# Group 0's roundings in turns, W1 in four transfers, group 1 two tiles at once, and the mean product of batch 1 at the end of group 2

## What is computed

```python
x_mean = jnp.mean(x, axis=1, keepdims=True)
fused = jnp.concatenate([x, x_mean * ones_L, hidden[:, None, :] * ones_L], axis=-1)
out = x + jax.nn.relu(jnp.einsum('bld,do->blo', fused, W) + b)
```

## Time and profile before

| | us |
|---|---|
| runs | 103.11, 103.53, 103.65 (median 103.53) |
| profiled execution | 103.63, of which the span of the trace is 101.7 |
| TensorE busy | 97.2 of 101.7 (96%), 523 matmuls |
| VectorE / ScalarE / GpSimd busy | 83.0 / 47.1 / 38.9 |
| DMA | 21.39 MB, mean 210 GB/s |

### The profile page before, as it was taken

The page is one execution under the profiler, slowest core; times in us unless marked ns, Lnnn a source line. Parts: engine busy times, 40 slices in busy tenths (PEclk is TensorE's granted clock), DMA queues, the critical chain, the costliest instruction groups (busy, mean ns, idle before and its releaser), DMA issues.

```text
span 101.7 us, 1713 instructions
## 1 busy us (share of the span) xinstructions
PE 97.2 (96%) x523; PEld 78.5 (77%) x523; DVE 83.0 (82%) x148; ACT 47.1 (46%) x116; POOL 38.9 (38%) x35
## 2 busy tenths in 40 slices
PE   5989999999999999999999999999999999999980
PEld 2348999988888786888888886888888886888870
DVE  3172789899899899999999984999999993996670
ACT  3285435895418279496397001874744003710000
POOL 1029800000000002999848500568578059950000
PEclk9999999999999999999999999999999999999999
DMA  1999999999999998999999388000591690299994
GB/s 38 269 303 290 273 268 282 273 251 266 318 256 231 269 251 221 246 234 226 345 331 286 106 195 219 0 0 0 113 267 32 134 259 20 67 283 273 248 325 144
DMA packets 35438, 21.39 MB, mean 210 GB/s; under 512 B 2020, under 2 KB 33128, under 8 KB 35432
## 3 DMA queue, kind: packets, MB, share of 16 engines
q1 hardware_dynamic: 33848, 20.13, 77.4%
q10 hardware_dynamic: 1584, 1.18, 3.9%
HBM read 12.91 MB, written 8.39 MB: 209 GB/s over the span
## 4 chain that ended last, share of the span: by engine, by line
PE 90%; DMA 4%; ACT 1%; DVE 1%; ACTq 0%; issue 0%
PE ps_y L472 77%; PE ps_y L573 4%; PE ps_y L575 4%; PE ps_y L574 4%; DMA xa<-in_x_dram 4%; PE ps_mean L491 1%; PE ps_const L540 1%; ACT xh L267 1%; DVE ps_xt L341 1%; ACT w1h L260 1%; DVE w L462 0%; ACTq L160 0%; PE ps_y L596 0%
## 5 line engine op out<-in xcount | busy, mean ns | idle before, releaser
L240 POOL TENSOR_TENSOR xa<-xa,back 128x512 f32 (+1 forms) x26 | 33.5, 1318 | 44.7 <-DVE back L354 44.7
L472 PE MATMUL ps_y<-xh,w1h 128*128 (+2 forms) x128 | 43.6, 368 | 0.4 <-ACT w1h L260 0.3
L472 PE MATMUL ps_y<-xl,w1h 128*128 (+2 forms) x128 | 43.0, 363 | 0.0
L472 PE MATMUL ps_y<-xh,w1l 128*128 (+2 forms) x128 | 42.8, 363 | 0.0
L267 ACT ACTIVATE xh<-ps_xt 128x512 fp32r<-128x512 f32 (+1 forms) x36 | 19.7, 549 | 17.4 <-DVE ps_xt L341 17.4
L472 PEld LDWEIGHTS ps_y<-xh,w1h 128*128 128x128 f32 x128 | 22.6, 189 | 5.4 <-issue 1.1
L347 DVE TENSOR_TENSOR xl<-ps_xt,xh 128x512 fp32r<-128x512 f32 (+1 forms) x36 | 22.1, 617 | 4.9 <-ACT xh L267 4.9
L472 PEld LDWEIGHTS ps_y<-xh,w1l 128*128 128x128 f32 x128 | 22.6, 189 | 3.8
L472 PEld LDWEIGHTS ps_y<-xl,w1h 128*128 128x128 f32 x128 | 22.7, 189 | 3.6
L341 DVE STREAM_TRANSPOSE ps_xt<-xa 128x512 f32<-128x512 f32 (+1 forms) x36 | 22.3, 642 | 3.6 <-DMA xa<-in_x_dram 3.3
L285 ACT ACTIVATE relu_t<-ps_y,bias 128x512 f32<-128x512 f32 x20 | 13.5, 686 | 16.8 <-DVE bias L388 15.3
(11 more groups left out here) (35 smaller groups left out, 37.1 us busy)
## 6 DMA issues: line engine op xcount, KB each, us to landing
xa<-in_x_dram SPq DMA_DIRECT2D x60, 128.0 KB, 3.8
out_dram<-xa SPq DMA_DIRECT2D x28, 256.0 KB, 4.1
w<-in_L_cond_W_dram SPq DMA_DIRECT2D x4, 256.0 KB, 5.5
w<-in_L_cond_W_dram SPq DMA_DIRECT2D x2, 512.0 KB, 6.7
w<-in_x_dram SPq DMA_DIRECT2D x4, 256.0 KB, 4.6
out_dram<-w SPq DMA_DIRECT2D x3, 256.0 KB, 3.4
xa<-in_x_dram ACTq DMA_DIRECT2D x4, 128.0 KB, 4.4
w<-in_L_cond_W_dram SPq DMA_DIRECT2D x4, 64.0 KB, 3.4
```

Of the source, the lines that this page charges most:

```text
L240: nc.gpsimd.tensor_tensor(rows, rows, back[:, t], ALU.add).then_inc(added, 1)
L472: return nc.tensor.matmul(ps_y[:, t, ls], lhs, rhs, start=start, stop=stop, skip_group_check=True)
```

## The change

1. ScalarE rounds piece k and block k of W1 in turns from k = 0. Of block 0 it rounds only tiles 0 and 1; VectorE rounds tiles 2 and 3 between its transposes of pieces 1 and 2. TensorE waits for VectorE's half at t = 2 of its first step, GpSimd before its first remainder.
2. W1's blocks 2 and 3 are loaded in transfers of their own, with a semaphore each. The second half of group 0's x is loaded by SyncE alone, behind W1. The cond transfers move behind x1, and the transpose of cond on VectorE behind group 1's pieces.
3. TensorE computes group 1's tiles 0 and 1 together, k outside, then tiles 2 and 3 one by one. ScalarE saves tile 1 of group 0 earlier.
4. `mean_bias(1)` moves from behind tile 2 to the end of group 2, and `sum_bias(1)` on VectorE from in front of turn_back(2) to in front of turn_back(4). Two more tiles (0 and 1 of group 2) are saved, into W1's own buffer, which is no longer read by then; ScalarE does it in front of relu(4), and TensorE's group 3 waits for these saves where it waited for their relus.
5. TensorE's loop over groups 3 to 6 is written out.

```diff
--- before.py
+++ after.py
@@ -65,7 +65,7 @@
     tiles = [(g, t) for g in range(LAST) for t in range(NK)]
 
     DVE_ADDS = 2
-    SAVED = H * NK
+    SAVED = H * NK + 2
 
     def steps_of_x(n, ahead):
 
@@ -84,6 +84,9 @@
 
 
     bias_line = nc.dram_tensor("bias_line", [D], F32).ap()
+
+
+    DVE_T = NK // 2
 
     def by_tile(rows):
         return rows.rearrange("p (j t m) -> p t j m", j=NQ, t=NK)
@@ -135,12 +138,12 @@
 
         x0_landed = [sem(f"x0_landed{h}") for h in range(2)]
         x_landed = [sem(f"x_landed{g}") for g in range(G)]
-        w1_landed = [sem(f"w1_landed{k}") for k in range(NK - 1)]
+        w1_landed = [sem(f"w1_landed{k}") for k in range(NK)]
         w2_landed, w3_landed = sem("w2_landed"), sem("w3_landed")
         cond_landed, b_landed = sem("cond_landed"), sem("b_landed")
         stored = sem("stored")
         warm_zeroed, cond_zeroed, ones_set = sem("warm_zeroed"), sem("cond_zeroed"), sem("ones_set")
-        w1h_ready, w1l_ready = sem("w1h_ready"), sem("w1l_ready")
+        w1h_ready, w1h_rest_ready, w1l_ready = sem("w1h_ready"), sem("w1h_rest_ready"), sem("w1l_ready")
         cond_spread, const_summed, const_ready = sem("cond_spread"), sem("const_summed"), sem("const_ready")
         halves_summed, bsum_ready = sem("halves_summed"), sem("bsum_ready")
         w2x_step = sem("w2x_step")
@@ -176,6 +179,10 @@
 
         last_x = w3[:].rearrange("p r k o -> p (r k) o")
 
+        def place(n):
+
+            return w1[:, n - RELU_RING] if RELU_RING <= n < SAVED else relu_t[:, n % RELU_RING]
+
         def store_last(eng, r, cols, added_steps):
             eng.wait_ge(last_added, added_steps)
             eng.dma_start(out_rows[LAST, :, r, cols], last_x[:, r, cols]).then_inc(stored, 16)
@@ -187,12 +194,13 @@
             load_x0(sp, 0, LOW)
             load_w1(sp, 0, 1, LOW)
             load_w1(sp, 1, 2, LOW)
-            load_w1(sp, 2, NK, LOW)
-            load_x0(sp, 1, LOW)
+            load_w1(sp, 2, 3, LOW)
+            load_w1(sp, 3, 4, LOW)
+            load_x0(sp, 1, ORDER)
+            load_x(sp, 1, ORDER)
             sp.wait_ge(cond_zeroed, 1)
             for j in range(NQ):
                 sp.dma_start(cond_c[Q * j:Q * j + B], cv[j].rearrange("b (m k) -> b m k", k=CK)).then_inc(cond_landed, 16)
-            load_x(sp, 1, ORDER)
             load_x(sp, 2, ORDER)
             load_w2(sp, ORDER)
             for j in range(NQ):
@@ -230,8 +238,10 @@
             nc.gpsimd.memset(cond_c[:], 0.0).then_inc(cond_zeroed, 1)
 
             for k in range(NK):
-                pool.wait_ge(w1_landed[min(k, NK - 2)], 16 * NQ)
+                pool.wait_ge(w1_landed[k], 16 * NQ)
                 pool.wait_ge(w1h_ready, k + 1)
+                if k == 0:
+                    pool.wait_ge(w1h_rest_ready, 1)
                 nc.gpsimd.tensor_tensor(as_tiles(w1l[:, k]), by_tile(w1[:, k]), as_tiles(w1h[:, k]),
                                         ALU.subtract).then_inc(w1l_ready, 1)
             def residual(g, t, n):
@@ -252,12 +262,13 @@
             nc.scalar.activation(act_warm[:], ones[:, 0:1], ACT.Relu)
             load_w1(act, 0, 1, HIGH)
             load_w1(act, 1, 2, HIGH)
-            load_w1(act, 2, NK, HIGH)
-            load_x0(act, 1, HIGH)
+            load_w1(act, 2, 3, HIGH)
+            load_w1(act, 3, 4, HIGH)
 
             def w1_high(k):
-                act.wait_ge(w1_landed[min(k, NK - 2)], 16 * NQ)
-                nc.scalar.activation(as_tiles(w1h[:, k]), by_tile(w1[:, k]), ACT.Copy).then_inc(w1h_ready, 1)
+                act.wait_ge(w1_landed[k], 16 * NQ)
+                ts = slice(0, NK if k else DVE_T)
+                nc.scalar.activation(as_tiles(w1h[:, k])[:, ts], by_tile(w1[:, k])[:, ts], ACT.Copy).then_inc(w1h_ready, 1)
 
             def x_high(n):
 
@@ -269,36 +280,35 @@
 
             def save(n):
                 act.wait_ge(y_ready, n + 1)
-                nc.scalar.activation(relu_t[:, n % RELU_RING], ps_y[:, n % Y_BANKS], ACT.Copy).then_inc(y_saved, 1)
+                if n >= RELU_RING:
+                    act.wait_ge(w1l_ready, NK)
+                nc.scalar.activation(place(n), ps_y[:, n % Y_BANKS], ACT.Copy).then_inc(y_saved, 1)
 
             def relu(n):
                 g, t = tiles[n]
-                products, slot = ps_y[:, t], n % RELU_RING
+                products = ps_y[:, t]
                 if n < SAVED:
                     act.wait_ge(y_saved, n + 1)
-                    products = relu_t[:, slot]
+                    products = place(n)
                 else:
                     act.wait_ge(y_ready, n + 1)
                     act.wait_ge(turned_back, n + 1 - RELU_RING)
                 if n % (H * NK) == 0:
                     act.wait_ge(bias_ready, g // H + 1)
-                nc.scalar.activation(relu_t[:, slot], products, ACT.Relu,
+                nc.scalar.activation(place(n), products, ACT.Relu,
                                      bias=bias[:, g // H, t, g // H:g // H + 1]).then_inc(relu_done, 1)
 
-            x_high(0)
-            x_high(1)
-            w1_high(0)
-            w1_high(1)
-            for k in range(2, NK):
+            for k in range(NK):
                 x_high(k)
                 w1_high(k)
             for n in range(NK, pieces_to(H) - 2):
                 x_high(n)
             save(0)
+            save(1)
             x_high(pieces_to(H) - 2)
             x_high(pieces_to(H) - 1)
-            for n in range(1, NK):
-                save(n)
+            save(2)
+            save(3)
             n_x = pieces_to(H)
             x_high(n_x)
             x_high(n_x + 1)
@@ -314,8 +324,12 @@
             x_high(n_x + 2)
             x_high(n_x + 3)
             n_x += NK
-            assert n_x == pieces_to(SLOTS) and SAVED == 2 * NK
+            assert n_x == pieces_to(SLOTS) and SAVED == 2 * NK + 2
             for n in range(len(tiles)):
+                if n == 4:
+
+                    save(2 * NK)
+                    save(2 * NK + 1)
                 relu(n)
                 for _n in range(steps_of_x(n, 2)):
                     x_high(n_x)
@@ -351,7 +365,7 @@
                 dve.wait_ge(relu_done, n + 1)
                 if n >= BACK_RING:
                     dve.wait_ge(added, n + 1 - BACK_RING)
-                nc.vector.transpose(back[:, n % BACK_RING], relu_t[:, n % RELU_RING].rearrange("p (lb om) -> p lb om", om=Q)
+                nc.vector.transpose(back[:, n % BACK_RING], place(n).rearrange("p (lb om) -> p lb om", om=Q)
                                     ).then_inc(turned_back, 1)
 
             def mean_terms(b):
@@ -404,12 +418,18 @@
             for p in (0, P // 2):
                 nc.vector.memset(two_rows[p:p + 1], 1.0).then_inc(rows_set, 1)
             turn_x(0)
-            turn_and_split(0, pieces_to(1))
+            turn_x(1)
+            dve.wait_ge(w1_landed[0], 16 * NQ)
+            nc.vector.tensor_copy(as_tiles(w1h[:, 0])[:, DVE_T:NK], by_tile(w1[:, 0])[:, DVE_T:NK]).then_inc(w1h_rest_ready, 1)
+            x_low(0)
+            turn_x(2)
+            turn_and_split(1, 2)
+            turn_and_split(2, pieces_to(1))
+            turn_x(pieces_to(1))
+            turn_and_split(pieces_to(1), pieces_to(H))
 
             dve.wait_ge(cond_landed, 16 * NQ)
             nc.vector.transpose(cond_t[:], cond_c[:].rearrange("p m k -> p k m")).then_inc(cond_spread, 1)
-            turn_x(pieces_to(1))
-            turn_and_split(pieces_to(1), pieces_to(H))
             turn_x(pieces_to(H))
             turn_and_split(pieces_to(H), pieces_to(H + 1))
             mean_terms(0)
@@ -424,7 +444,7 @@
             mean_terms(1)
             n_x = pieces_to(SLOTS)
             for n in range(len(tiles)):
-                if n == 2:
+                if n == NK:
                     sum_bias(1)
                 elif n == NK * (H + 1):
                     sum_bias(2)
@@ -515,6 +535,8 @@
                             mm(t, ls, w1l[:, k, t], xh[:, 0, k, ls], stop=True).then_inc(y_ready, 1)
                         break
                     for t in range(NK):
+                        if half == 0 and k == 0 and t == DVE_T:
+                            pe.wait_ge(w1h_rest_ready, 1)
                         mm(t, ls, w1h[:, k, t], xh[:, 0, k, ls], start=(half == 0 and k == 0))
                     pe.wait_ge(xl_ready, NK * half + k + 1)
                     for t in range(NK):
@@ -526,7 +548,16 @@
                 if half == 0:
                     group0_low(half, NK - 1)
 
-            for t in range(NK):
+
+            for k in range(NK):
+                pe.wait_ge(xl_ready, pieces_to(1) + k + 1)
+                for t in (0, 1):
+                    if k == 0:
+                        pe.wait_ge(y_saved, t + 1)
+                    last = product(1, k, t)
+                    if k == NK - 1:
+                        last.then_inc(y_ready, 1)
+            for t in (2, 3):
                 pe.wait_ge(y_saved, t + 1)
                 tile(1, 1, t)
 
@@ -551,21 +582,21 @@
```

(28 more changed lines are left out.)

## The result

The changed kernel takes 104.26 us (median of 21 runs, 103.50 to 105.08) against 103.61 us for the kernel before (21 runs, 103.03 to 104.52). The ratio is 1.0064, 95% interval 1.0041 to 1.0086: **slower by 0.6%**, where 0.7% faster was forecast. The range of 102.4 to 103.8 does not hold it.

The account below looks back on a forecast made before the run. The prediction took TensorE's almost unbroken matmuls as the bound, with gain only before 9.8 us: 103.63 - 0.71 (0.39 first product, 0.32 W1's block 2) = 102.92, with the median 0.10 lower: 102.85 us, range 102.4 to 103.8.

Parts of the forecast that it names:

- Step 7: TensorE's loop written out: the back edge lies in a stretch without a gap, so nothing to gain.
- The sum's sentence: After the front: nothing behind 9.8 us absorbs the 0.71 us gain, since TensorE is the chain to the end.
- Step 6: Later mean product and two more saves: relu(10) has 0.7 us slack, saves are done in time, nothing on the path.
- Steps 1 and 2: Front: roundings in turns start the first product 0.39 us earlier; loading W1's block 2 by itself removes a stall, 0.32.
- Step 3: Second half of group 0's x on SyncE: 3.8 us latency taken, landing at 10.7, 0.9 us of slack.
- Step 4: SyncE's longer queue: w3 issued 1.9 us later, lands at 33.0, wanted at 33.4, no stall.
- Rival B: w3 lands late: stall of 0.3 to 0.8 us before the constant's products, 103.1 to 103.6 us; chance 0.20.
- Step 5: Group 1, two tiles at once: no time by itself, but avoids a 0.3 us stall and so keeps the front's gain.
- Rivals C: W1's block 2 lands no earlier, so 0.63 of the 0.71 us is lost: 103.5 us; chance 0.10.
- D: Second half of group 0's x keeps its 5.7 us latency: stall 0.9 us, 103.7 us; chance 0.09.
- E: A SyncE issue blocked 3 us in front of w3: stall up to 3.7 us, 103.7 to 106.5 us; chance 0.09.
- parts 1 to 5: Edits of the prediction's first five steps: all but the mean product's move, two more saves and written-out loop; 0.71 us gain.

Follow-up runs that it names:

- e4: Kernel before with only TensorE's loop over groups 3 to 6 written out; 104.23 us, 1.0074.
- d1: e4 with 5 needless waits ahead of each of the last group's first 12 products, behind the fetch; 104.00 us, 1.0064.
- d2: e4 with 11 needless waits ahead of each product of group 2, so the block comes earlier; 103.36 us, 0.9998.
- b2: e4 with 30 more instructions, needless waits in groups 1 and 2 ahead of the fetch; 103.72 us, 1.0013.
- b1: Kernel before, loop kept, with 24 needless waits ahead of each tile of group 1 and 10 ahead of each product of group 2; 104.00 us, 1.0058.
- e3: Kernel before with the mean product's move, the two more saves and the loop written out; 104.71 us, 1.0101.
- b4: Changed kernel with 30 needless instructions in groups 1 and 2, ahead of the fetch; 103.16 us, 0.9965.
- b3: e1 with 30 needless instructions in groups 1 and 2, ahead of the fetch; 103.02 us, 0.9948.
- e1: Changed kernel with batch 1's mean product in the middle of tile 3 of group 2, not at the group's end; 103.77 us, 0.9989.
- d3: c1 with batch 1's mean product moved by one product, into tile 3 of group 2; 103.30 us, 0.9974.
- c4: b3 with group 1 computed tile by tile as before; 103.46 us, 1.0003.
- f1: e1 with 11 needless waits ahead of each product of group 2; 102.96 us, 0.9937.
- c1: Changed kernel with the mean product's move and two saves undone and TensorE's loop kept; 103.26 us, 0.9994 to the kernel before.
- c2: e1 with the turn-backs of two more tiles ahead of the mean's terms on VectorE; 104.55 us, 1.0134.
- c3: b3 with the turn-backs of two more tiles ahead of the mean's terms on VectorE; 103.36 us, 0.9990.

## Why the prediction was wrong, by its own steps

**Step 7, the loop written out, costed at 0, is the step that failed.** It asked only whether the back edge stalls TensorE, found that it doesn't (the trace before still says so), and stopped there. What the longer program adds is one more block of instructions, and what that costs hangs on when it comes: at 87 us some 0.7 us (e4: 1.0074; d1: 1.0064), at 77 to 85 us nothing (d2: 0.9998; b2: 1.0013). It shows in the landing of the last store. The page of before showed three such packets, in a row that was passed over; dividing the program's length by the 256 instructions that the Trainium skill gives to a block (same section), and asking which stretch the next fetch falls in, would have found it. (902 instructions had three packets, 1030 in b1 and 1077 four, which fits.) The Trainium skill's rule on taken branches, named beside the step, speaks for unrolling and led away from it; the other one of that section ("Runtime: NRT & Kernel Launch", Instruction fetch mechanics), that crossing into a new block is mostly hidden, holds for a block at 77 or 85 us here and not for one at 87.

**The sum's sentence that nothing behind 9.8 us absorbs the gain, since TensorE is the chain to the end,** was wrong in two places. The chain ends in stores, not in TensorE; SyncE's wait for the last 128 KB was never looked at, and it varies from 1.4 to 2.7 us among these profiles, more than the whole forecast gain. And the chain left TensorE at 41.8 us.

**Step 6, "nothing on the path", was wrong by about 0.3 us.** It followed relu(10) and the saves, which were right (TensorE has no such wait in the profile). It did not follow VectorE's queue to its end in that group of work: the terms of batch 2, which had 1.17 us of slack before. The product's end moved from about 40.0 to 42.2, VectorE stood idle 0.62, and 0.73 us reached the terms. TensorE's lead of 0.61 and VectorE's lag of 0.73 together are 1.34, against 1.17 of slack: a wait of 0.17; 0.24 was measured. The step had what was needed: its own lead of 0.71 and its own "about 1 us later" for VectorE come to 1.7 against the 1.17 that the trace before shows, a wait of 0.5. e3 against e4 puts it at 0.3%, b4 against b3 at 0.2%, each within overlapping intervals, e1 at 0.4 to 0.75%.

**Steps 1 and 2 were right, a little large.** First product 6.79 (forecast 6.67), fourth step 9.25 without a stall (9.15), half 1 at 12.61 (12.51): 0.61 us of the 0.71. Over the profiles of all kernels here, half 1 starts at 13.18 in the mean with the old order (8 kernels) and at 12.63 with the new (12), so 0.55 is typical. The stall that step 2 removes differs between executions: with the old order the fourth step starts anywhere from 9.53 (d2) to 10.20 (b2). **Step 3**: x's second half landed in 3.4 to 3.6 us, better than the 3.8 taken. **Step 4**: w3 was issued at 25.3 and 25.8, 1.8 later as forecast, and landed in 5.1 to 7.3; no stall in the profile of the changed kernel nor in nine others, one of 0.6 us in d3. Rival B was priced right, and one profile in eleven does not contradict the 0.20 it got. **Step 5** holds (c4). Rivals C, D and E did not come about; the slower side had been given to E, a blocked issue, and came by a mechanism that no rival named.

**The sum with the measured terms**, in per cent: the best version, without a late block and with the mean product in the middle, is -0.6 (f1); a late block +0.4 to +1.4 (four pairs; 0.66 between d1 and d2); the mean product at the end of group 2 +0.2 to +0.4. That gives 0.0 to +1.2, and +0.64 was measured: it fits, but is no sharp check, and the changed kernel itself is in one of the pairs. That parts 1 to 5 are worth 0.5 to 0.6 us is thus shown with the loop out and the block early (b3, f1); with the loop kept, c1 and d3 gave 0.1 and 0.3%, with intervals that touch those of b3 and f1. Why they are less is open. So is how one packet of 16 KB, fetched 12 us before the last store is issued, makes that store land 0.5 us later: only its place was varied, and no profile shows stores queued behind it.

## What to carry to other kernels

When a change makes an engine's program longer, count its instructions and look on the page at the packets of the instruction queue: one more block cost nothing measurable ahead of the last stores and 0.7% where they start, and a few needless instructions moved it. When a step on which another engine waits is moved later, follow that engine's queue until the first thing that the critical engine wants from it, and subtract the critical engine's new lead from the slack as well. And look at the last store's wait before saying that a gain in front reaches the end.

## What was not expected of the hardware

It is an instruction block's place in time that seems to cost, not its being fetched: each takes about 1 us of one of 16 DMA engines, and only the one at 87 us goes with a longer wait for the last store, even though the share of the engines in use was lower around it (17% to 24%) than around the harmless one in b2 (62%).

Some operations of VectorE last until GpSimd's addition is over. The 128x4 addition of `bsum` took 0.12 us at 36.18 with GpSimd idle, and 0.98 at 56.89 in the kernel before, where it ended at 57.87 and GpSimd's addition (56.57 + 1.29) at 57.86; at 78.14 it took 0.70 and ended at 78.84, GpSimd's (77.53 + 1.29) at 78.82. In c2 it ended at 79.73, as the first of the two additions shown above did (about 79.7), and the multiplication by a column lasted from 79.77 to 81.25, past the end of the second (80.96), 1.48 us (1.47 in c3), for 0.49 in all other kernels, where GpSimd was idle at that place. The transposes beside them took their usual 0.6 to 0.7. That the one waits for the other is read from these ends; no run changed it alone.

And executions of one kernel differ by up to 1.5 us (103.37 to 104.90 in d1), where the front differs by 0.6 between profiles (half 1 at 12.27 to 12.88 with the new order) and the wait for the last store by 1.3 (1.4 to 2.7).
